# Graph sums and a mixture of experts on one core: key rounds with fewer chunk groups, filler matmuls, and another order in the last slot

## The reference, cut to what matters

```
edge_index = stack([src, dst])
# network 0: two layers of: mean over incoming edges of x[src] @ W_l + b_l + x @ W_r, relu between
x = layernorm(x + L0(x))
# network 1: h = x @ W_in + b_in, then three layers:
agg    = segment_sum(h[src], dst) / deg
logits = concat([h, agg]) @ router_W[l] + router_b[l]       # 8 experts, the best 2 are taken
h      = h + sigmoid(h @ conf_W[l] + conf_b[l]) * (gated sum of 2 experts of agg)
x = layernorm(x + h @ W_out + b_out)
```

## Time and profile before

| | us |
|---|---|
| median of 3 runs | 2031.82 |
| lowest and highest | 2031.15, 2037.95 |
| the profiled execution, its own time | 2040.89 |
| its span on the core | 2039.1 |
| TensorE busy in it | 1772.0 |
| VectorE, ScalarE, GpSimd busy | 892.9, 829.7, 619.0 |

### The profile page before, as it was taken

How to read it: one execution, slowest core, us unless ns; L and a number is a source line. 1 busy time by engine, 2 the same in 40 slices (tenths; PEclk the granted TensorE clock), 3 DMA queues, 4 the chain that set the end, 5 groups by cost and what they waited for, 6 DMA issues and landing times.

```text
span 2039.1 us, 30707 instructions
## 1 busy us (share of the span) xinstructions
PE 1772.0 (87%) x9747; PEld 1376.1 (67%) x9748; DVE 892.9 (44%) x2593; ACT 829.7 (41%) x1404; POOL 619.0 (30%) x593
## 2 busy tenths in 40 slices
PE   3856666589999998999979998999979998999974
PEld 2545555445566654888868877888868777888864
DVE  6589999834344335533321113433321113433324
ACT  6156666634322222333326563333336663333321
POOL 1044444300000033444430231544430221644430
PEclk9866666689999999999999998999989997999986
DMA  6970000034566783354448551454458541544441
GB/s 145 341 265 0 0 0 0 24 128 173 197 204 222 244 312 123 74 114 74 71 73 283 196 192 44 83 111 72 68 107 284 184 165 43 96 68 74 74 114 51
DMA packets 162537, 259.54 MB, mean 127 GB/s; under 512 B 27776, under 2 KB 136043, under 8 KB 162424
## 3 DMA queue, kind: packets, MB, share of 16 engines
q1 hardware_dynamic: 125960, 206.09, 31.5%
q0 software_dynamic: 36464, 51.98, 14.5%
HBM read 149.08 MB, written 108.94 MB: 127 GB/s over the span
## 4 chain that ended last, share of the span: by engine, by line
PE 76%; DVE 12%; issue 5%; ACT 3%; DMA 2%; DVEq 1%; SPq 1%; POOL 0%; ACTq 0%; POOLq 0%
PE psum L1685 17%; PE psum L1696 16%; PE psum L1507 14%; PE psum L1594 13%; DVE arena L764 7%; PE psum L1651 2%; PE psum L1487 2%; PE psum L1674 2%; PE psum L1422 2%; PE psum L1454 2%; PE psum L1452 1%; PE psum L1645 1%; PE psum L1718 1%; DVEq L764 1%; PE psum L1478 1%
## 5 line engine op out<-in xcount | busy, mean ns | idle before, releaser
L669 POOL DMA_INDIRECT h_rows<-arena,idx x192 | 312.9, 1629 | 420.5 <-DVE arena L1115 374.7
L1359 ACT ACTIVATE arena<-psum,b1c 128x256 f32<-128x256 f32 x384 | 181.8, 473 | 462.5 <-PE psum L1685 462.5
L1685 PE MATMUL psum<-arena 128*128 128x256 f32 x1536 | 360.6, 389 | 6.7 <-ACT arena L1356 6.7
L1696 PE MATMUL psum<-arena 128*128 x1536 | 347.4, 379 | 0.0
L1685 PEld LDWEIGHTS psum<-arena 128*128 128x128 f32 x1536 | 281.1, 193 | 70.9 <-ACT arena L1359 18.7
L1507 PE MATMUL psum<-arena 128*128 128x384 bf16 (+1 forms) x1875 | 316.9, 326 | 0.5 <-ACT arena L1243 0.2
L1696 PEld LDWEIGHTS psum<-arena 128*128 128x128 f32 x1536 | 284.6, 190 | 34.8
L764 DVE TENSOR_TENSOR arena<-arena 125x1200 bf16<-125x1200 bf16 (+1 forms) x300 | 282.4, 1008 | 20.4 <-PE psum L1454 19.5
L1507 PEld LDWEIGHTS psum<-arena 128*128 128x128 bf16 x1875 | 181.5, 98 | 125.7 <-ACT arena L1246 3.2
L644 POOL DMA_INDIRECT xs_d<-arena,pos x150 | 146.3, 976 | 390.4 <-DVEq L946 348.4
L1113 DVE TENSOR_TENSOR arena<-psum,arena 128x256 f32<-128x256 f32 x192 | 80.9, 421 | 378.2 <-PE psum L1696 377.0
(11 more groups left out here) (252 smaller groups left out, 1751.2 us busy)
## 6 DMA issues: line engine op xcount, KB each, us to landing
arena<-adj_d SPq DMA_DIRECT2D x54, 800.0 KB, 4.5
ring<-adj_d SPq DMA_DIRECT2D x46, 800.0 KB, 4.5
xs_d<-zrow SPq DMA_DIRECT2D x8, 3432.0 KB, 27.3
arena<-xs_d SPq DMA_DIRECT2D x96, 264.0 KB, 2.8
adj_d<-arena SPq DMA_DIRECT2D x25, 800.0 KB, 4.4
h_rows<-zrow SPq DMA_DIRECT2D x1, 8192.0 KB, 39.3
h_new<-h_rows SPq DMA_DIRECT2D x12, 640.0 KB, 8.0
arena<-h_rows SPq DMA_DIRECT2D x10, 640.0 KB, 6.7
```

The source lines that it names most:

```text
L669: pool.indirect_dma_start(h_rows, bass.IndirectOffsetOnAxis(ap=idx[:, j % 2, h:h + 1], axis=0), ybuf[:, j % 2, h], None, compute_op=ALU.ad ...
L1359: act.activation(hid[:, j % 2, f], psum[:, 5 + f % 2, 0:M], ACT.Relu, bias=b1c[:, bass.ds(at_b1[j % LOAD] + f, 1)]).then_inc(b_hidf, 1)
L1685: mm = pe.matmul(psum[:, 5 + f % 2, 0:M], w1s[:, j % 2, f // 2, kt, f % 2 * P:(f % 2 + 1) * P], xsT[:, j % 2, kt], start=(kt == 0), stop=( ...
L1696: mm = pe.matmul(psum[:, h, 0:H], hid[:, j % 2, f, h * P:(h + 1) * P], w1f[:, bass.ds(at_w2 + f * H, H)], start=(f == 0), stop=(f == FT - 1))
```

## The change

It has five parts.

1. *Groups.* Rounds 0 and 3 use four of the eight chunk groups: round 0 the first four, round 3 the last four, on the engine that multiplies and on the one that compares. In round 3 the one-row matmul starts from chunk 400 and not from chunk 0 (`starts[:, 1]`), and two more one-row matmuls add the constant 400 (`first[:, 8]`).
2. *Zero matmuls.* Ahead of round 0 stand 14 matmuls of zeros with 512 columns. They wait for the 15th linked step of VectorE (`KEYS_NEAR`), the one of L710 in the kernel before.
3. *Spare matmuls.* Where a layer's `aggregate` begins (p = 3 and 4), 36 matmuls with 512 columns whose result nobody reads go to bank 7. They stand ahead of the wait for the last slot's outputs.
4. *The last slot's halves in turn.* For slot 31 `slot_output` goes through all four pieces of half 0, then through those of half 1.
5. *Order of conversions.* ScalarE converts slices 0 to 2 of the second piece after unit 3 of the new `h`, where slices 0 and 1 stood before it.

```
+        first = carve([10, CE], BF16, 1)
+        starts = first[:, 0:8].rearrange("o (h k) e -> o h k e", h=2)
...
+        HJ = CJ // 2
+        MID = HJ * CP
+        KEYS_NEAR = 15
+        def moving(m):
+            return range(0, HJ) if m == 0 else range(HJ, CJ) if m == T // TP - 1 else range(CJ)
```

VectorE's part; the other three keys' copies change alike:

```
+            link(v.memset(first[:, 8], float(MID)))
...
-            link(v.tensor_copy(first[:, 0], key_a[0:1, 0, 0]))
+            link(v.tensor_copy(starts[:, :, 0], key_a[0:1, 0, 0:CJ:HJ]))
...
             def compare(m):
...
-                for j in range(CJ):
+                for j in moving(m):
```

ScalarE's part, after the last slot of a layer:

```
-                        for s in {2: (0, 1), 3: (2,), 4: (3, 4)}.get(u, ()):
+                        for s in {3: (0, 1, 2), 4: (3, 4)}.get(u, ()):
```

TensorE's part, the key rounds first:

```
+            pe.wait_ge(s_v, KEYS_NEAR)
+            for _ in range(14):
+                pe.matmul(psum[:, 7, :], zeros_b[:, :], ones_b[:, :], start=True, stop=True)
             for m in range(T // TP):
...
+                late = int(moving(m)[0] > 0)
                 for o, keys in ((h, (2, 3)), (h + 1, (1,)), (h + 2, (0,))):
                     for k in keys:
-                        pe.matmul(psum[0:CE, o, 0:TP], first[0:1, k], ones_b[0:1, 0:TP], start=(k == keys[0]), stop=False)
-                        for j in range(CJ):
+                        pe.matmul(psum[0:CE, o, 0:TP], starts[:, late, k], ones_b[0:1, 0:TP], start=(k == keys[0]), stop=False)
+                        if late and k == 3:
+                            pe.matmul(psum[0:CE, o, 0:TP], first[:, 8], ones_b[0:1, 0:TP], start=False, stop=False)
+                        for j in moving(m):
```

In `aggregate(p, b)`:

```
                 if b == 0:
+                    pe.wait_ge(a_rankf, blk(p, 0))
+                    pe.wait_ge(e_early[1], 16 * (p - 2))
+                    for _ in range(36):
+                        pe.matmul(psum[:, 7, :], tri[:, :], early[:, 1, 0, 0:512], start=True, stop=True)
                     pe.wait_ge(b_yt, 2 * SLOTS * (p - 2))
```

In `slot_output(p, j, at_w2)`:

```
-                for f in range(FT):
+                by_f = [(f, h) for f in range(FT) for h in range(2)]
+                by_h = [(f, h) for h in range(2) for f in range(FT)]
+                for f, h in by_h if j == SLOTS - 1 else by_f:
```

More of the change, by code:

```diff
@@ L134, in build @@
         ones_b = carve([512], BF16)
-        first = carve([4, CE], BF16, 1)
+        first = carve([10, CE], BF16, 1)
+        starts = first[:, 0:8].rearrange("o (h k) e -> o h k e", h=2)
         last_w = carve([CJ], I32, CP)
@@ L704, in _ @@
             link(v.tensor_tensor(delta[:, 1], key_a[:, 1], key_a[:, 0], ALU.subtract))
-            link(v.tensor_copy(first[:, 1], key_a[0:1, 0, 0]))
+            link(v.tensor_copy(starts[:, :, 1], key_a[0:1, 0, 0:CJ:HJ]))
             link(v.tensor_scalar(key_a[:], edge_dst[:], 5, 3, ALU.logical_shift_right, ALU.logical_shift_left))
             link(v.tensor_tensor(delta[:, 2], key_a[:, 1], key_a[:, 0], ALU.subtract))
-            link(v.tensor_copy(first[:, 2], key_a[0:1, 0, 0]))
+            link(v.tensor_copy(starts[:, :, 2], key_a[0:1, 0, 0:CJ:HJ]))
             link(v.tensor_scalar(key_a[:], edge_dst[:], 2, 7, ALU.logical_shift_right, ALU.bitwise_and))
             link(v.scalar_tensor_tensor(delta[:, 3], key_a[:, 1], 1.0, key_a[:, 0], ALU.add, ALU.subtract))
-            link(v.tensor_copy(first[:, 3], key_a[0:1, 0, 0]))
+            link(v.tensor_copy(starts[:, :, 3], key_a[0:1, 0, 0:CJ:HJ]))
             link(v.tensor_scalar(last_w[:, :], edge_dst[:, 0, :, CE - 1], 2, None, ALU.logical_shift_right))
@@ L1417, in _ @@
                 h = 4 * (m % 2)
+                late = int(moving(m)[0] > 0)
                 for o, keys in ((h, (2, 3)), (h + 1, (1,)), (h + 2, (0,))):
                     for k in keys:
-                        pe.matmul(psum[0:CE, o, 0:TP], first[0:1, k], ones_b[0:1, 0:TP], start=(k == keys[0]), stop=False)
-                        for j in range(CJ):
-                            pe.matmul(psum[0:CE, o, 0:TP], delta[:, k, j], past[:, m % 2, j], start=False, stop=(j == CJ - 1 and k == keys[-1]))
-                for j in range(CJ):
-                    mm = pe.matmul(psum[0:CE, h + 3, 0:TP], ones_b[0:CP, 0:CE], past[:, m % 2, j], start=(j == 0), stop=(j == CJ - 1))
+                        pe.matmul(psum[0:CE, o, 0:TP], starts[:, late, k], ones_b[0:1, 0:TP], start=(k == keys[0]), stop=False)
+                        if late and k == 3:
+                            pe.matmul(psum[0:CE, o, 0:TP], first[:, 8], ones_b[0:1, 0:TP], start=False, stop=False)
+                        for j in moving(m):
+                            pe.matmul(psum[0:CE, o, 0:TP], delta[:, k, j], past[:, m % 2, j], start=False, stop=(j == moving(m)[-1] and k == keys[-1]))
+                if late:
+                    pe.matmul(psum[0:CE, h + 3, 0:TP], first[:, 8], ones_b[0:1, 0:TP], start=True, stop=False)
+                for j in moving(m):
+                    mm = pe.matmul(psum[0:CE, h + 3, 0:TP], ones_b[0:CP, 0:CE], past[:, m % 2, j], start=(j == 0), stop=(j == moving(m)[-1]))
                 mm.then_inc(s_gath, 1)
@@ L1690, in slot_output @@
                 J = slot(p, j)
-                for f in range(FT):
+                by_f = [(f, h) for f in range(FT) for h in range(2)]
+                by_h = [(f, h) for h in range(2) for f in range(FT)]
+                for f, h in by_h if j == SLOTS - 1 else by_f:
                     pe.wait_ge(b_hidf, 4 * J + f + 1)
[L1693 to L1699, removed]
+                    if J and f == 0:
+                        pe.wait_ge(b_yt, 2 * (J - 1) + h + 1)
+                    mm = pe.matmul(psum[:, h, 0:H], hid[:, j % 2, f, h * P:(h + 1) * P], w1f[:, bass.ds(at_w2 + f * H, H)],
+                                   start=(f == 0), stop=(f == FT - 1))
+                    if f == FT - 1:
+                        mm.then_inc(b_y, 1)
             def final(b):
```

## The result

The changed kernel took 2016.3 us (median of 5, 2014.1 to 2019.5) against 2031.8 (median of 5, 2031.2 to 2040.6): the ratio is 0.991, with a 95% interval from 0.989 to 0.994. A second sample, on another occasion, gave 0.992 (0.990 to 0.994). The kernel is 0.9% faster, clear of noise, and the range of 1997 to 2022 held the time, but the forecast of 2006 was 10 us too low. The profiled execution took 2015.76 us, 25.1 less than the one of before, where the sum said 33.2.

What follows compares the result with a forecast made beforehand. TensorE was taken as the bound, at half clock in the key rounds. From the profiled 2040.9 us, -27.4 - 2 x 1.4 - 3.0 = -33.2 gave 2007.7; less 1.5, the forecast was 2006 us, range 1997 to 2022.

Steps and rivals of the forecast that it cites:

- Bound of the kernel before: Key rounds: TensorE is the longest part of the first 90 us, at 1.2 GHz from 30.8 to about 78 us.
- Part 1: Key rounds 0 and 3 with fewer matmuls: 5.27 and 5.9 us at 2.4 GHz, 9.5 and 10.5 at 1.2 GHz.
- Part 2, the clock: Zero matmuls ahead of the key rounds raise the clock; round 0 starts at 31.6, stage ends at 60.0 us, -27.4 us.
- Part 2, the supersteps: Superstep loop starts as much earlier as the key rounds end; nobody waits for the clearing beside it.
- Rival B: Supersteps: if any transfer beside them slows them, starting 27 us sooner loses 9 us, time 2015; chance 0.12.
- Part 3: Changes between layers: 36 spare matmuls take 7.7 us of 10.2 idle, aggregation starts fast; 1.4 us at each of two.
- the 2.9 us: Start of aggregation: its first 25 matmuls would take 5.7 us instead of 8.55, but not all of this gain arrives.
- piece 3: Aggregation: ScalarE's conversion of this piece is late next; its matmuls, begun at 1088.64, can begin at 1087.2 us.
- Part 4: Last slot: GpSimd's indirect DMA starts 1.0 us sooner (0.6 to 1.3) at three places, -3.0 us.
- Part 5: Aggregation, ScalarE's order of conversions: taken as 0 (bounds -0.5 and +0.8), since a later conversion decides anyway.
- Execution and median: Profiled execution was 9.1 us above the median of three; one key round less at 1.2 GHz explains 7.6 of it.
- The 1.5 us taken off: Whole time: the rest of the profiled execution's distance above the median, subtracted from the sum of 2007.7 us.

Runs made afterwards that it cites:

- one-row matmuls first: Kernel before, with each key round's four one-row matmuls put ahead of its 40 others, which then run without a gap; ratio 0.997 (0.995 to 0.998).
- halves alone: Kernel before, with only the last slot's output done half by half; last slot to next stage took 9.2, 9.1 and (final) 10.7 us.
- zero matmuls alone: Kernel before, with only the 14 zero matmuls added ahead of key round 0, all rounds full; ratio 0.997 (0.995 to 0.999).
- spare matmuls alone: Kernel before, with only the 36 spare matmuls added at the start of `aggregate`; its 125th matmul came after 30.5 and 30.3 us instead of 31.2.

## Why the prediction came out as it did

- **Bound of the kernel before** (1.2 GHz in the key rounds though the profile's column says 1.00): right. The record's first rise, at 78.0 us, is at the place where the matmuls become faster (2.86 us for eight in the rounds before, 1.50 in the one behind).
- **Part 1:** right. Rounds of 5.2 and 5.9 us stood against 5.3 and 5.9.
- **Part 2, the clock:** right, rise within the zero matmuls in all nine traces that have them (at 27.0 to 31.7 us). The stage ended at 58.9 (-28.5) against 60.0 (-27.4), since the fillers began at 25.95 us and not 26.3, and round 0 at 30.6 and not 31.6. What I took as weighing against it, that rounds 0 and 1 had the same stretch and no rise, was chance: the rise comes in round 0, 1 or 2. The work of the key rounds, busy as it reads, was broken by the one-row matmuls; where it wasn't (one-row matmuls first) the clock rose 6.4 us after it began.
- **Part 2, the supersteps:** this step failed, and it is most of the miss: the clearing cost 7.0 us in the loop and 1.0 ahead of it, and the profiled execution was 8.1 us above the 2007.7 of the sum. "The clearing is beside it and nobody waits for it there": nobody waits for its end, but TensorE's register loads are slowed by it, 3.3 us instead of 1.6. Rival B had the price (9 us, measured 7.0) and half the mechanism: it is any transfer of the clearing, not that of `h_rows`. From 106 to 116 us, the rows on which I leant for `h_rows`, two loads took 1.7 us beside the clearing of `xs_d`; why these two were fast is open.
- **Part 3:** the clock stayed up as said, the spare matmuls took 7.7 us as said, and the first 25 of `aggregate` 5.9 for 5.7. The 1.4 us a change were 0.7 and 1.7, parts 3 and 5 together, and some 0.5 in the mean for each of them alone. So most of the 2.9 us that the faster start was taken to give didn't arrive, as said, and the term of 1.4 was too large for part 3. What I had named as late next, piece 3, is not what took the gain: in the first change TensorE waited 0.24 us for its conversion, and 1.2 us for the split of `h` between pieces 0 and 1, which the prediction did not have.
- **Part 4:** the term of 1.0 us was 1.2, 1.3 and 1.5 (12.05 against 10.56), by the mechanism named (GpSimd starts 0.39 us after the landing before).
- **Part 5:** some 0.5 us a change, taken as 0.
- **Execution and median:** one or two key rounds at 1.2 GHz less can explain the distance, as I said; two traces with unchanged key rounds show that the rise moves so, and what it is worth behind the loop (5 to 11 us). The 1.5 us taken off beyond it weren't there: the changed kernel's profiled execution was at its median.
- **Gather** took 1.5 us more; the clock was at 1.2 GHz for 3.4 us (452.4 to 455.9), behind a wait of 2.5 us. The second trace of the changed kernel has a wait of 2.9 us there, no fall of the clock and 378.1 us. But five traces of its variants have the fall, and took 379.1 to 381.0 us. So it comes back; what decides it is open.

The sum with the measured terms: -28.5 + 1.0 (first superstep) + 7.0 + 1.5 - 4.0 (part 4) - 2.4 (parts 3 and 5) + 0.3 (all else) = -25.1 us.

## What to carry to other kernels

When a stage is moved in time, list the transfers that run at fixed times, and read from the trace how long each kind of instruction of the stage takes beside them, register loads too: here TensorE's took 1.62 us without the clearing and mostly 3.1 to 3.9 beside it, and 7.0 of the 27.5 us by which the first superstep came sooner went back to them.

Where a matmul stage starts at half clock, filler matmuls ahead of it are worth a run. Here 14 of them brought the end of the key rounds from 87.3 us (79.1 and 71.8 in two other traces of the same rounds) to 65.0, and with part 1 to 58.9. Let them reach up to the stage's first matmul: with a gap of 2.1 us behind them the stage ended at 69.0, where part 1 without any filler had 68.8.

If a stage stays at half clock though it reads as busy, look for an odd matmul every few. The key rounds of the kernel before, with a one-row matmul as every ninth, were slow up to 78.0 us (61.0 and 45.2 in two other traces). With the odd ones put together the clock rose at 38.5 us and the stage ended at 65.5, without filler, in the one trace there is.

Before making a result sooner, look up which earlier DMA its user also waits for. Half 0 of slot 31 was ready at 1039.60 us, but the landing at 1040.23 decided, and part 4 gave 1.2 to 1.5 us at each of three places.

## What the runs showed of the hardware that was not expected

- A register load (TENSOR_LOAD, 24 values) by TensorE took 1.62 us without transfers, mostly 3.1 to 3.9 beside 340 GB/s of clearing, now and then only 1.7 to 2.8 or as much as 4.6, and 5.5 to 5.9 once in each of the 13 traces with the clearing beside the loop, near the clearing's end.
- With a one-row matmul as every ninth TensorE stayed at 1.2 GHz for 15 to 47 us (from 30.6 to 45.2 with the halves alone, 30.8 to 78.0 in the kernel before), though it reads as busy all the time; with the one-row matmuls first it was 7.9 us (from 30.6 to 38.5). Once at 2.4 GHz the same rounds stayed there (28.9 to 65.0 with the zero matmuls alone).
- How long the clock outlasts the work differs. 2.1 us of idle time and five matmuls lost it; 2.4 us (spare matmuls alone) and 2.9 (gather, second trace) kept it. Behind the key stage's last matmul it fell 1.0 us later in the changed kernel's trace and 3.7 with the one-row matmuls first.
- The clock rose during the matmuls of zeros in nine of nine traces (27.0 to 31.7 us); the five without them have the rise at 38.5 to 78.0.
- One chip ran `aggregate` slower. With the spare matmuls alone, on that chip, early and later in the first `aggregate`:

```profile
1070.00:1130.00 60.00, 57.52 (x279) 1.00 0.83 299
1150.00:1280.00 130.00, 123.58 (x489) 0.74 0.29 95
```

The granted clock falls to 0.74 in the mean while TensorE is busy 95% of the time. The first `aggregate` took 218 us there and 180 to 181 on the other chips, which had 1.00 in all of it but at most its first 6 us. All eight `aggregate` stages in the four traces from this chip took 209 to 219 us. What limits it no run here tells.
